# High one-hot rows of a weighted sum: stored to DRAM in the first sum, loaded again in the second

## The reference

```python
e_exp = jnp.exp(e - e_max[dst])
denom = jax.ops.segment_sum(e_exp, dst, num_segments=n)
a = e_exp / denom[dst]
out = jax.ops.segment_sum(a[:, None] * nfeat[src], dst, num_segments=n)
```

```python
messages = x[src] * edge_weights[:, None]
out = jax.ops.segment_sum(messages, tgt, num_segments=x.shape[0])
```

## Time and profile before

| | us |
|---|---|
| median of 3 runs (4649.11 to 4655.57) | 4654.58 |
| the profiled execution | 4662.1 |
| its span, first to last instruction | 4660.3 |
| first weighted sum, starts of its first L1653 and of its last count store | 1638.4 to 2801.9 |
| second weighted sum, first L1644 to last L1684 | 3624.3 to 4626.2 |

### The profile page before, as it was taken

How to read it: one execution, slowest core, us unless ns; L and a number is a source line. 1 busy time by engine, 2 the same in 40 slices (tenths; PEclk the granted TensorE clock), 3 DMA queues, 4 the chain that set the end, 5 groups by cost and what they waited for, 6 DMA issues and landing times.

```text
span 4660.3 us, 227804 instructions
## 1 busy us (share of the span) xinstructions
PE 3742.0 (80%) x103291; PEld 3166.1 (68%) x103291; DVE 3623.5 (78%) x4577; ACT 1871.6 (40%) x2437; POOL 928.1 (20%) x810
## 2 busy tenths in 40 slices
PE   5631885949728589999989997998998799999996
PEld 4631774948728567777777776997997567777675
DVE  5974686786875899989989985555555999999996
ACT  5300102001010056656656664664664444444443
POOL 0565667652253162000000000000000000000000
PEclk8975695967858899999999998998998899999998
DMA  6743252632514411111111113553553000000000
GB/s 153 263 140 51 72 171 73 182 113 77 151 22 137 123 50 62 58 56 64 61 55 61 62 55 118 177 176 126 179 179 104 8 11 10 11 10 10 11 10 18
DMA packets 240229, 404.31 MB, mean 87 GB/s; under 512 B 110259, under 2 KB 167861, under 8 KB 239525
## 3 DMA queue, kind: packets, MB, share of 16 engines
q1 hardware_dynamic: 213928, 383.16, 26.4%
q0 software_dynamic: 25472, 10.79, 1.2%
q10 hardware_dynamic: 184, 0.08, 0.0%
HBM read 287.89 MB, written 110.03 MB: 85 GB/s over the span
## 4 chain that ended last, share of the span: by engine, by line
PE 70%; DVE 11%; issue 6%; POOL 4%; ACT 2%; DMA 1%; DVEq 0%; SPq 0%; ACTq 0%
PE psum L1123 19%; PE psum L1096 17%; PE psum L1163 13%; PE psum L930 10%; PE psum L1084 3%; POOL heads_d L620 2%; POOL gath L628 2%; PE psum L898 2%; PE psum L872 1%; PE psum L1172 1%; DVE space L1653 1%; DVE space L1433 1%; PE psum L886 1%; DVE V L1418 1%; DVE small L1381 1%
## 5 line engine op out<-in xcount | busy, mean ns | idle before, releaser
L784 ACT COPY space<-psum 128x784 f32<-128x784 f32 x1184 | 949.2, 819 | 705.2 <-PE psum L1096 701.1
L1096 PE MATMUL psum<-space 64*128 64x49 bf16 x56832 | 892.5, 184 | 160.7 <-issue 138.5
L1096 PEld LDWEIGHTS psum<-space 64*128 64x128 bf16 x56832 | 807.0, 94 | 295.6 <-issue 253.0
L1123 PE MATMUL psum<-space,X 128*64 128x256 f32 x7252 | 955.1, 392 | 19.0 <-issue 17.2
L1653 DVE TENSOR_TENSOR space<-space 128x2352 bf16<-128x2352 bf16 x592 | 812.0, 1372 | 0.0
L930 PE MATMUL psum<-table,space 128*128 128x56 bf16 x24300 | 673.8, 189 | 114.0 <-DVE space L1303 77.8
L930 PEld LDWEIGHTS psum<-table,space 128*128 128x128 fp8e4 x24300 | 660.7, 96 | 127.0 <-issue 119.4
L1645 DVE TENSOR_TENSOR space<-space,V 128x2048 bf16<-128x2048 bf16 x592 | 718.5, 1214 | 0.0
L1123 PEld LDWEIGHTS psum<-space,X 128*64 128x64 f32 x7252 | 534.8, 139 | 224.5 <-issue 42.6
L1163 PE MATMUL psum<-space 128*128 128x192 bf16 x7252 | 629.1, 247 | 11.8 <-ACT space L817 11.8
L1300 DVE TENSOR_REDUCE space<-psum 128x1512 f32 (+1 forms) x300 | 518.7, 1731 | 133.1 <-PE psum L930 128.6
(11 more groups left out here) (286 smaller groups left out, 2951.4 us busy)
## 6 DMA issues: line engine op xcount, KB each, us to landing
space<-adj_d SPq DMA_DIRECT2D x148, 784.0 KB, 4.3
space<-onehots SPq DMA_DIRECT2D x240, 432.0 KB
adj_d<-space SPq DMA_DIRECT2D x222, 192.0 KB
onehots<-space SPq DMA_DIRECT2D x60, 432.0 KB, 3.4
space<-digit_rows SPq DMA_DIRECT2D x60, 378.0 KB
adj_d<-space SPq DMA_DIRECT2D x74, 208.0 KB
space<-cw_d SPq DMA_DIRECT2D x37, 160.0 KB, 2.2
cw_d<-space SPq DMA_DIRECT2D x4, 1184.0 KB, 13.2
```

The lines of the kernel that those rows point to most:

```text
L784: nc.scalar.copy(A[:, h, :, b * P:(b + 1) * P].rearrange("p a (w s) -> p w a s", w=2)[:, :, :, c:c + UC], psum[:, 2 + 2 * (k % 2):4 + 2 * ...
L1096: mm = nc.tensor.matmul(psum[:, 2 + 2 * e + w, c * NB:(c + 1) * NB], ohlo[lo:hi, ring, col // 2, :, col % 2], ohw[lo:hi, ring, r, col // 2 ...
L1123: mm = nc.tensor.matmul(pb[6][half:half + F, 0:2 * P], X[:, a, :], A[:, 1 - h, a, :], start=(a < 2), stop=(a >= NB - 2))
```

## The change

In the first sum SP stores the high one-hot rows of every step to a DRAM tensor `hot_d` (196 KB a step, 296 steps). In the second sum DVE no longer makes them; SP loads them in transfers of four steps (784 KB, two a block) into the memory of `adj` (`hot_back`), one block ahead, and DVE's multiplication L1653 reads them from there. DVE gets a wait in the first sum (a step's rows may be overwritten only when the store of two steps before has landed) and one in the second, ahead of steps 0 and 4. SP's program of the first sum is ordered anew, with the stores of the rows between those of the counts. ACT and PE keep their programs; one semaphore pair has a new name.

```diff
+        hot_d = dram("hot_d", (NDB, 2, P, HS // 2, HC * NB), BF16)
...
+        hot_back = adj.rearrange("p h a s -> p (h a s)").bitcast(BF16).rearrange("p (h t x) -> p h t x", h=2, t=HS // 2)
...
+            def store_hot(i, h, t):
+
+                sp.wait_ge(hi_made, i * (2 * HS) + (h * HS + t + 1))
...
+                sp.dma_start(hot_d[at, half, :, step, :].rearrange("d p x -> (d p) x"),
+                             ohhi[:, t % 2, :, :, :].rearrange("p s a e -> p (s a e)")).then_inc(oh_saved[t % 2], 16)
+
+            def load_hot(i, h, half):
...
+                sp.dma_start(hot_back[:, half, :, :].rearrange("p t x -> p (t x)"),
+                             hot_d[at, half].rearrange("d p t x -> (d p) (t x)")).then_inc(half_loaded[half], 16)
...
+            def pair_out(i, h, more=True, last=False):
+
+                for t in (3, 4, 5):
+                    store_hot(i, h, t)
+                store_counts(i, h, 0, (0, 1))
+                store_hot(i, h, 6)
+                store_counts(i, h, 0, (2, 3))
+                store_hot(i, h, 7)
                 if more:
...
+                    next_codes(0, i, h)
+                if not last:
+                    store_hot(i, h + 1, 0)
+                store_counts(i, h, 1, (0,), last)
+                if not last:
+                    store_hot(i, h + 1, 1)
+                store_counts(i, h, 1, (1, 2), last)
+                if not last:
+                    store_hot(i, h + 1, 2)
+                store_counts(i, h, 1, (3,), last)
+
+            def pair_in(i, h, more=True, last=False):
+
+                if not last:
+                    for half in range(2):
+                        sp.wait_ge(hot_ready, i * (2 * HS) + (NDB * HS + h * HS + (half + 1) * (HS // 2)))
+                        load_hot(i, h + 1, half)
+                if more:
+                    next_codes(1, i, h)
 
             def pairs(n):
 
+                one = pair_in if n else pair_out
+                if n:
+                    sp.wait_ge(mm_psum, 2 * NMG)
+                    for half in range(2):
+                        sp.wait_ge(oh_saved[half], 16 * (NCH // OR + NDB * HS // 2))
+                        load_hot(0, 0, half)
+                else:
+                    for t in range(3):
+                        store_hot(0, 0, t)
...
-                nc.vector.tensor_tensor(ohhi[:, ring, :, :, :], pairs_of(cw[:, h, P + t * HC:P + (t + 1) * HC], NB), table(NB), ALU.is_equal).then_inc(hi_made, 1)
+                if n == 0:
+                    if not first:
+                        dve.wait_ge(oh_saved[ring], i * (16 * HS) + 16 * (NCH // OR + h * (HS // 2) + t // 2))
+                    nc.vector.tensor_tensor(ohhi[:, ring, :, :, :], pairs_of(cw[:, h, P + t * HC:P + (t + 1) * HC], NB), table(NB), ALU.is_equal).then_inc(hi_made, 1)
                 nc.vector.tensor_tensor(ohlo[:, ring, :, :, :], pairs_of(cw[:, h, t * HC:(t + 1) * HC], P), table(P), ALU.is_equal)
-                dve.wait_ge(hi_made, done + 1)
                 if n == 0:
+                    dve.wait_ge(hi_made, done + 1)
...
+                    hot = ohhi[:, ring, :, :, :]
+                else:
+                    half = t // (HS // 2)
+                    if t % (HS // 2) == 0:
+                        dve.wait_ge(half_loaded[half], i * 32 + 16 * (NRB + h + 1))
+                    hot = hot_back[:, half, t % (HS // 2), :].rearrange("p (s a e) -> p s a e", s=UC, e=2)
...
-                each = ohhi[:, ring, :, :, :].unsqueeze(1).to_broadcast([P, 3, UC, NB, 2])
+                each = hot.unsqueeze(1).to_broadcast([P, 3, UC, NB, 2])
```

More of the change, by code:

```diff
@@ L513, in codes_in, with store_counts @@
                     sp.dma_start(cw[:, h, 0:codes_of[n]], cw_d[n, h, :, 0:codes_of[n]]).then_inc(cw_loaded[h], 16)
-            def store_counts(i, h, b, last=False):
-                for q, (lo, hi) in enumerate(STORES):
+            def store_counts(i, h, b, quarters, last=False):
+                for q in quarters:
+                    lo, hi = STORES[q]
                     sp.wait_ge(adj_made, i * (4 * GU) + ((2 * h + b + 1) * GU + (0 if last else q)))
-                    sp.sem_inc(sp_ok, 1)
+                    if not isinstance(i, int):
+                        sp.sem_inc(sp_ok, 1)
                     at = slice(4 * i + 2 * h + b, 4 * i + 2 * h + b + 1) if isinstance(i, int) else bass.ds(i * 4 + (2 * h + b), 1)
@@ L522, in store_counts @@
                                  adj[:, b, lo:hi, :].rearrange("p a s -> p (a s)")).then_inc(adj_stored[b], 16)
-            def pair(n, i, h, more=True):
-                if n == 0:
-                    store_counts(i, h, 0)
-                if more:
[L529 to L535, removed]
@@ L537, in pairs @@
-            def pairs(n):
+            def store_hot(i, h, t):
+                sp.wait_ge(hi_made, i * (2 * HS) + (h * HS + t + 1))
+                if not isinstance(i, int):
+                    sp.sem_inc(sp_ok, 1)
+                at = slice(2 * i + h, 2 * i + h + 1) if isinstance(i, int) else bass.ds(i * 2 + h, 1)
+                half, step = t // (HS // 2), t % (HS // 2)
+                sp.dma_start(hot_d[at, half, :, step, :].rearrange("d p x -> (d p) x"),
+                             ohhi[:, t % 2, :, :, :].rearrange("p s a e -> p (s a e)")).then_inc(oh_saved[t % 2], 16)
@@ L539, in pairs @@
                 with sp.Fori(0, NDB // 2 - 1) as i:
                     for h in range(2):
[L541 to L544, removed]
+                        one(i, h)
+                one(NDB // 2 - 1, 0)
+                one(NDB // 2 - 1, 1, more=False)
+                one(NDB // 2, 0, more=False, last=True)
             codes_in(0)
@@ L560, in apply_loads @@
                         sp.wait_ge(cast_dve, NRB)
-                    sp.dma_start(adj8[:, h, :], adj_d[h]).then_inc(adj_loaded[h], 16)
+                    sp.dma_start(adj8[:, h, :], adj_d[h]).then_inc(half_loaded[h], 16)
                 with sp.Fori(1, NRB // 2) as i:
```

22 lines of the change are left out of this document (15 added, 7 removed).

## The result

The changed kernel takes 4749.6 us (median of 4 runs, 4736.4 to 4760.3) against 4655.1 us of the kernel before (4 runs, 4649.1 to 4661.5): the ratio is 1.0203, with a 95% interval of 1.0182 to 1.0225. It is 2% slower, 94.5 us. The prediction was 4655 us with a range up to 4686. The profiled execution took 4748.1 us (span 4746.3), 86 us more than that of before.

The account below looks back on a forecast made before the run. The prediction took PE's own matmuls to bound the second sum, with stalls at its instruction packets' edges. Its terms, -4.3 - 3.6 + 4 + 4 = 0.1 us, meant no change: 4655 us, range 4636 to 4686.

Parts of the forecast that it names:

- forecast 4.3: Second sum's first block, before mixing: nine DVE steps each 0.48 us shorter without the comparison, a gain of 4.3 us.
- forecast 3.6: Second sum's later blocks: PE's waits for DVE shrink, a gain of 3.6 us, ends 0 and 7.2.
- forecast: half: Second sum's later blocks: stalls for instruction packets take back half of what DVE's shorter step gives up.
- the price of the loads: Second sum: loads share DMA engines with PE's instruction packets, costing 4 us, bounds 0 and 40.
- A: Rival: packets wait out a load's engine share in the dense stretch, up to 51 us slower (4706), middle 4677; chance 0.28.
- a time share above 2%: Sign in the second sum: instruction packets' time share of the engines above 2% would show A.
- the other sign: Sign in the second sum: the prediction is wrong if issue stalls exceed 2 us a block.
- My bound from above: Second sum's loads: if each packet waits for a load's whole engine share, 0.75 us a load, 40 us at most.
- the dense stretch: PE's products of steps 6, 7 and the next block's 0, nearly without mixing; said to ask for 588 records in 5.1 us.
- the stores were forecast at 4 us: First sum: 296 stores of 196 KB delay PE's instruction packets by 4 us, bounds 0 and 19.
- rival C: First sum, slower: DVE waits for stores if issue and landing exceed 5.9 us, up to 1 us a step; chance 0.02.
- Rival B: Second sum, faster: issue stalls shrink with DVE's step, 21 us, 4634; chance 0.28 including the upper end of own gains.

Follow-up runs that it names:

- run 1: Changed kernel without the second sum's loads after the first block's two, every block multiplying block 0's rows: 4655.5 us, ratio 1.0000 to the kernel before.
- run 12: As run 11, but the bytes of a block's two loads go as eight transfers of 196 KB: 4697.3 us, ratio 1.0095 to the kernel before.
- run 11: As run 10, but DVE doesn't wait for the loads; SP waits for the previous block's loads: 4783.4 us, ratio 1.0275 to the kernel before.
- run 3: Changed kernel with a block's second load moved into the mixing phase of the block that uses it: 4707.5 us, ratio 1.0104 to the kernel before.
- run 4: Changed kernel with one step to a load (196 KB, eight a block): 4684.6 us, ratio 1.0070 to the kernel before.
- run 2: Changed kernel with loads and stores, but DVE makes the rows again in the second sum and multiplies these: 4740.3 us, ratio 1.0181 to the kernel before.
- run 10: As run 2, but both loads of a block are issued together at the block's end: 4808.7 us, ratio 1.0283 to the kernel before.
- run 9: Kernel before with PE's second sum as a loop over pairs of blocks: 4812.2 us against 4681.5 on that chip, ratio 1.0280.
- run 5: Changed kernel's first sum with its stores, second sum as in the kernel before, without loads: 4660.3 us, ratio 1.0030 to the kernel before.
- 8: Changed kernel without loads after the first block's, mixing spread evenly, 7 terms behind each of steps 0 to 6: ratio 1.0028 to the kernel before.
- 6: Kernel before with PE's mixing spread evenly, 7 terms behind each of steps 0 to 6: ratio 0.9996 to the kernel before.

## Why the prediction was wrong

The reading of what bounds the kernel held. The comparisons are off the critical path: in run 1 their removal changes the first block by 3.3 us (forecast 4.3) and the rest of the second sum by 4.2 us, which is no more than scatter (forecast 3.6). The packet's stalls took over nearly all that DVE's waits had been (7.6 of 8.1 us; forecast: half). The forecast of no change had this right and missed a loss of 94.5 us, because of one step.

**The step that failed** is the price of the loads: "The nearest row is the first sum's, so I take from it: 0.03 us for seven packets and 36 blocks is 7.6 us at full price, half paid, 4 us." The changed kernel's second sum is 76.8 us longer than that of run 1, which lacks only the loads, and its first block 2.9 us: the loads cost 80 us where this term has 4, about 1.1 us a load. Two things were wrong in it.

- The row measured the wrong quantity. It gives the time that an instruction packet takes once it moves, and this stayed what it was: 214 packets at 1.6% of 16 engines in 900 us are 1.08 us each, against 1.12 before. What grew is the time before it starts, which no packet's duration contains: the same 241 packets are spread over 1017.1 us in place of 944.5, the longest distance between two of them is 6.9 us in place of 5.5, and PE stands until one has come. So my sign for A, a time share above 2%, could not show it either; the other sign did, with 95.7 us of stalls in 36 blocks, 2.7 a block where I had put the limit at 2. The row also came from count stores, whose rows in memory are 1536 bytes, and run 12 against run 11 shows that such small ones do little harm; the loads' rows are 6272 bytes. The rival, A, had the mechanism right. Of the place it had half: run 3 still loses 34.8 us with both loads in the mixing phase. My bound from above (0.75 us a load, 40 us) was nearer the truth than the value taken, but too low as well.
- The clock was not in the sum. Of the 72.6 us above before, 33.4 are PE being busy longer for the same matmuls, with a granted clock of 0.94 for 0.98; 39.2 are idle time. I counted what a stall costs while it lasts and nothing for the stretch behind it. An estimate from rows agrees: 99 us more at the lower level cost 35 us if they held products alone (2.18 us a group for 1.42), and 47 if mixing alone (3.68 us for 1.95 in the first block of before, at 3652.69 and 3657.68).

Runs in which PE executes the same second sum, in the order of their longest stall before the products:

| | longest stall, us | PE busy, us | granted clock |
|---|---|---|---|
| run 1, no loads | 1.8 | 872.6 | 0.99 |
| run 4, small loads | 2.2 | 878.1 | 0.99 |
| before | 2.3 | 878.1 | 0.98 |
| run 3, late load | 2.4 | 888.9 | 0.98 |
| run 12, eight together | 2.9 | 888.1 | 0.97 |
| run 2, loads alone | 3.9 | 901.1 | 0.95 |
| changed | 3.9 | 911.5 | 0.94 |
| run 11, two together | 4.3 | 914.4 | 0.93 |
| run 10, DVE late | 4.5 | 933.2 | 0.90 |
| run 9, loop | 4.6 | 919.3 | 0.91 |

Run 9 has no loads, and in run 10 most of PE's idle time is a wait for DVE. So the loads as such aren't what lowers the clock; what these runs share is that PE stood idle before. No run changed the length of the stalls and nothing else.

One reading of the prediction was off as well. It has the dense stretch ask for 588 records in 5.1 us from 4048.28. The 588 include step 6's products, which began at 4046.81 (the row shown above), so they take 6.6 us. The stretch is still the densest, and the conclusion stands.

The sentence on the Trainium skill's arbitration rule (DMA: Bandwidth & Descriptors, Queues, rings and completion order), that an engine changes queues only after a whole packet, can now be weighed: run 11 against run 12, and the packet that started after 108 of the load's 128, agree with its direction. How much an engine finishes before it changes queues, no run here shows. I had named the rule and given the rival 0.28 because one row spoke against it.

**The first sum:** the stores were forecast at 4 us, with 19 as the bound. Run 5 measures 14 us (6 to 22). No DVE wait for a store shows, as forecast, and rival C is out. That the cause is the same as with the loads is not shown: PE's stalls before the products are more in total in the first sum of the changed kernel (57.2 us in 74 against 51.2 in 65), but none is longer than before (1.6 us against 1.9).

**Rival B** (the stalls shrink with DVE's step) is refuted as a mechanism by run 1, whose stalls grew by 7.6 us, and DVE as the bound by the size of every gain seen. What the removed comparisons are worth in all is less certain: by the whole times run 1 (1.0000) is 0.3% below the stores alone of run 5 (1.0030), 14 us, but from different chips and with intervals that overlap, while 8 against 6 leaves nothing once the stores are taken off.

**In the first block** the changed kernel's gain was 0.4 us and not 4.3. From DVE's first start to ACT's first slot copy pass 3636.6 to 3691.8 us, 55.2, against 3624.3 to 3679.9, 55.6. DVE's steps are 2.43 us apart, but stalls of 2.73 and 2.43 us for packets eat it up:

```profile
3652.75 3.02 PE L1149 MATMUL psum<-space 64*128 64x49 bf16 x127 [2.73 <-issue]
...
3665.36 0.85 PE L1149 MATMUL psum<-space 64*128 64x49 bf16 x51 [2.43 <-issue]
```

Both come with the two loads for the next block, whose packets run from 3647.6 and from 3660.5 us. In run 1, without them, the same stretch takes 52.3 us (3628.6 to 3680.9), a gain of 3.3: this part of the forecast was sound but for the loads.

## What to carry to other kernels

In this kernel PE's written-out program has its own DMA traffic, and PE was slowed by transfers that nobody waited for (run 2). So before adding traffic beside such a stretch, look for idle "issue" time that moves by a constant from one round to the next. The duration of a packet tells nothing of how long it waited for its turn; take the spacing, or the stall on the engine. If the traffic must be there, try it in small transfers first: here that took the second sum's loss from 72.6 to 15.5 us with the same bytes (run 4). Moving a large load out of the densest stretch took it to 34.8 (run 3).

## What the runs showed of the hardware that I had not expected

- PE stood 51 us of 944 before its products, without any added traffic, and in this stretch each stall of over 1.5 us ended 2.4 to 2.9 us after the start of an instruction packet of 16 KB. Spreading the work evenly (59 stalls in place of 72) changed the whole time by no more than 0.25% either way.
- Loads of 784 KB lengthened the longest stall from 2.3 to 3.9 us; the same bytes in loads of 196 KB left it at 2.2. PE's clock was at its lower level, 0.50, behind the stall shown.
- A loop on PE with a body of 3500 records was slower than the same work written out, by 2.8%, and its clock fell to 0.91 without any load.
